# An adaLN mixer and mixture of experts on one core: z projection as split products, and every engine's step of the mixer in a new order

## The chip, the cores and the metric

The kernel runs on one core of a Trainium2 chip. A core has TensorE (matmuls into PSUM), VectorE, ScalarE and GpSimd, which run programs of their own and wait for each other by semaphores, and SyncE, which issues most DMA transfers. The metric is the device time of one execution in microseconds. Before the change the median of three runs was 5845.8 us (5838.91 to 5846.02).

## The reference, cut to what matters

Four sequences of 2048 tokens, width 512. Each token passes a state space mixer with a gate and then a mixture of 64 experts, eight per token, with one shared expert.

```python
h = _layernorm(x) * (1 + ca) + sa
xn = h * rsqrt(mean(h * h) + EPS) * norm_w
zxbcdt = xn @ in_proj_w.T             # z: 1024, xBC: 1024 + 2 * 128, dt: 16
conv = sum(pad[:, k:k + l, :] * conv_w[:, k] for k in range(4)) + conv_b
xBC = conv * sigmoid(conv)            # -> xs, B, C
dt = softplus(dt + dt_bias)
y = ssd(xs * dt, dt * A, B, C) + D * xs    # chunks of 128 tokens, a state carried from chunk to chunk
y = y * (z * sigmoid(z))
x = x + ga * (rmsnorm(y) * gnorm_w) @ out_proj_w.T
h2 = _layernorm(x) * (1 + cb) + sb
scores = sigmoid(h2 @ w_router)       # best 4 of 8 groups, best 8 experts
x = x + gb * (experts(h2) + shared(h2))
```

All arithmetic is fp32 in effect. Where the kernel wants fp32 quality at less TensorE work it splits both operands into a high and a low part of type fp32r and sums three products (high by high, high by low, low by high); the expert blocks did so before already, by the helper `split_products` (L1240).

## The kernel before, in words

The program has three parts. The function `mixer` walks over 64 chunks of 128 tokens and writes, per chunk, the residual `x1`, the normalised rows `h2` with their routing weights, and the lists of tokens per expert. In its spare moments it also splits one expert's weights per chunk into high and low parts. A short part builds tables from the lists. Then the expert blocks and a closing pass run.

In `mixer` each engine has a written-out `step`, called once per pass by `steps` (L493). One pass works on several chunks at once: `e` is the chunk two ahead (layer norm, `h`), `f` one ahead (the projections, the convolution, softplus of dt), `c` the current one (decay matrix `lm`, the products of the chunk, the state, the output product), `t` the last (`h2`, routing), `q` the one before (its list written). The order of the lines in `step` is the order of the engine's queue, so what waits at one line holds back all lines behind it on that engine; there is no scheduler.

A step of TensorE (L759 to L888) is: small products of `c` (L766), transposes of `xr` of `f` (L775), row sums of the decay matrix (L788), the xBC projection in four groups with dt (L811, L815), with the transposes of `h2` of `t` (L795) in between, the router (L825), the product inside the chunk `ydiag` (L832, 16 small matmuls), the product with the state `yoff` (L844), the new states (L853), the z projection (L860, eight fp32 matmuls of 512 columns), the transposes of `y` (L867), the two matmuls that rank the picked experts (L874), the transposes of xBC (L881) and the output product (L888).

VectorE multiplies `lm` by the masked B-C product (L956; the mask stands in PSUM, `half(4)`), applies three of four taps of the convolution (L982; ScalarE does the first), computes softplus as a series, and routes (L998 to L1037): a sigmoid's rest, best groups, best experts, up to `picked` (L1033), on which the rank matmuls wait. The series of softplus is laid between routing's operations. Then follow the sum of `y`, the gate, the state (L1043 to L1059), dt, the gate of z (L1086), the rank's keys, the split of weights (L518) and `x1` (L1109) with the statistics of its layer norm.

GpSimd (L580 to L654) forms `xg` (the gated `h` plus x), the reciprocal roots of both layer norms (`rs`, by a power) with the shifts `nm`, `xt` by the skip weights, `h2` and `h` (two operations each), the scaled rows `x2s`, the decayed state `tmp_s`, the scale `rr`, eight indirect DMAs that write the token list, and `r2`. SyncE's queue loads x and weights and stores x1, h2 and the split weights.

## Time and profile before

| what | value |
|---|---|
| median of three runs | 5845.8 us |
| profiled execution, its own time | 5848.36 us |
| its span from first to last instruction | 5846.6 us |
| mixer, 70 to 2640 us: TensorE busy | 2482.57 of 2570 us |
| VectorE, ScalarE, GpSimd busy in it | 2267.28, 1471.72, 1759.42 us |
| granted TensorE clock in it | 1.00 |
| expert blocks, 2700 to 5800 us: TensorE busy | 3031.78 of 3100 us |

"Busy" is the time in which an engine has at least one instruction in work; matmuls overlap, so that their starts tell more of their pace than their durations.
### The profile page before, as it was taken

How to read it: one execution, taken by the hardware profiler on the slowest of the kernel's cores; microseconds unless marked ns; L12 is line 12 of the kernel's file. 1: busy time of each engine (PE TensorE's matmuls, PEld its weight loads, DVE VectorE, ACT ScalarE, POOL GpSimd, SP SyncE). 2: the span in 40 equal slices, each digit the busy share in tenths (PEclk: the TensorE clock that was granted, in tenths of full speed). 3: DMA queues.
4: the chain of work that ended last, by engine and by line, in shares of the span. 5: the costliest groups of instructions: out<-in, count | busy, mean ns of one | idle time of the engine just before them, and what ended most of it. 6: DMA issues, size and time to landing. Idle time of an engine off the chain costs nothing.

```text
span 5846.6 us, 109797 instructions
## 1 busy us (share of the span) xinstructions
PE 5613.9 (96%) x28797; PEld 4286.0 (73%) x28798; DVE 3597.2 (62%) x10033; ACT 2627.2 (45%) x5588; POOL 3535.2 (60%) x2980
## 2 busy tenths in 40 slices
PE   5999999999999999994999999999999999999999
PEld 3666666666666666663888888887888888888887
DVE  4889888888898898883444444443444444444454
ACT  3555555555555555551333333333333333333322
POOL 2667667667676676673555555554555555555587
PEclk8999999999999999996999999999999999999999
DMA  5443444444444444343688788778678778878687
GB/s 203 163 149 144 162 155 152 154 143 163 158 145 165 147 146 160 145 151 133 138 225 222 183 202 224 164 177 238 138 182 203 160 161 218 208 199 201 132 277 248
DMA packets 340193, 1028.38 MB, mean 176 GB/s; under 512 B 57109, under 2 KB 61461, under 8 KB 339173
## 3 DMA queue, kind: packets, MB, share of 16 engines
q1 hardware_dynamic: 194232, 703.53, 32.9%
q0 software_dynamic: 145568, 321.56, 28.1%
q8 instruction: 118, 1.93, 0.1%
q14 instruction: 131, 1.07, 0.1%
q10 hardware_dynamic: 144, 0.29, 0.0%
HBM read 580.45 MB, written 444.74 MB: 175 GB/s over the span
## 4 chain that ended last, share of the span: by engine, by line
PE 52%; DMA 1%; POOL 0%; issue 0%; DVE 0%; SPq 0%; ACT 0%; POOLq 0%; ACTq 0%
PE bank L1244 45%; PE bank L1379 4%; PE bank L1386 2%; PE bank L1573 0%; PE bank L1582 0%; DMA w_lo<-lo_dram 0%; POOL acc_c L1555 0%; DMA h_c<-h_dram 0%; DMA lst_i<-list_dram,row 0%; DMA xg_e<-h_dram,ids 0%; POOL o_c L1559 0%; POOL acc_c L1546 0%; DMA acc_dram<-y_e,ids 0%; POOL lst_i L1172 0%; SPq L1531 0%
## 5 line engine op out<-in xcount | busy, mean ns | idle before, releaser
L1360 POOL DMA_INDIRECT acc_dram<-y_e,ids x576 | 910.4, 1580 | 1113.1 <-ACT y_e L1432 789.1
L1244 PE MATMUL bank<-w_hi,x_hi 128*128 (+1 forms) x2560 | 1056.1, 413 | 1.7 <-DVE x_lo L1647 1.2
L1244 PE MATMUL bank<-w_hi,x_lo 128*128 (+1 forms) x2560 | 1000.8, 391 | 0.0
L1244 PE MATMUL bank<-w_lo,x_hi 128*128 (+1 forms) x2560 | 1000.7, 391 | 0.0
L1450 DVE TENSOR_TENSOR h_lo<-bank,h_hi 128x256 fp32r<-128x256 f32 x576 | 243.8, 423 | 763.9 <-ACT h_hi L1421 763.7
L1432 ACT ACTIVATE y_e<-bank,xg_e 128x512 f32<-128x512 f32 x576 | 396.4, 688 | 698.4 <-PE bank L1244 698.4
L645 POOL DMA_INDIRECT list_dram<-tok_id,pos x512 | 594.9, 1162 | 156.0 <-issue 154.8
L1352 POOL DMA_INDIRECT xg_e<-h_dram,ids x576 | 571.0, 991 | 193.9 <-issue 174.9
L1426 ACT ACTIVATE th_f<-bank 128x256 f32<-128x256 f32 x576 | 221.3, 384 | 1011.2 <-PE bank L1244 1011.2
L811 PEld LDWEIGHTS bank<-xn_t,w_in 128*128 128x128 f32 x5120 | 587.8, 190 | 67.0 <-ACT btok L687 65.4
L811 PE MATMUL bank<-xn_t,w_in 128*128 128x131 f32 x5120 | 605.4, 276 | 14.8 <-ACT btok L687 14.1
L1459 DVE SCALAR_TENSOR_TENSOR hs_f<-th_f,bank 128x256 f32<-128x256 f32 x576 | 242.7, 421 | 600.1 <-ACT th_f L1426 599.8
L1244 PEld LDWEIGHTS bank<-w_hi,x_lo 128*128 128x128 f32 x2560 | 481.3, 188 | 103.5
L1244 PEld LDWEIGHTS bank<-w_hi,x_hi 128*128 128x128 f32 x2560 | 482.8, 189 | 83.4 <-DVE x_lo L1647 1.4
L1244 PEld LDWEIGHTS bank<-w_lo,x_hi 128*128 128x128 f32 x2560 | 484.1, 189 | 79.1
L982 DVE SCALAR_TENSOR_TENSOR acc<-bank,conv_w,acc 128x128 f32<-128x128 f32 x1920 | 505.7, 341 | 8.5 <-ACT acc L701 8.4
L1244 PE MATMUL bank<-w_hi,h_hi 128*128 (+1 forms) x1280 | 499.5, 390 | 2.2 <-DVE h_lo L1450 1.3
L1244 PE MATMUL bank<-w_hi,h_lo 128*128 (+1 forms) x1280 | 500.0, 391 | 0.0
L1244 PE MATMUL bank<-w_lo,h_hi 128*128 (+1 forms) x1280 | 498.1, 389 | 0.0
L888 PE MATMUL bank<-w_out,y_t 128*128 128x512 f32 x1024 | 452.4, 595 | 1.2 <-ACT y_t L751 1.2
L860 PE MATMUL bank<-w_in,xn_t 128*128 128x512 f32 x1024 | 450.0, 592 | 0.9 <-DVE acc L982 0.9
L1455 DVE TENSOR_TENSOR x_lo<-bank,x_hi 128x512 fp32r<-128x512 f32 x576 | 392.1, 681 | 8.7 <-ACT x_hi L1416 8.7
(247 smaller groups left out, 10448.6 us busy)
## 6 DMA issues: line engine op xcount, KB each, us to landing
hi_dram<-w_hi_m SPq DMA_DIRECT2D x130, 768.0 KB, 3.3
lo_dram<-w_raw SPq DMA_DIRECT2D x130, 768.0 KB, 4.8
w_hi<-hi_dram SPq DMA_DIRECT2D x130, 768.0 KB, 7.4
w_lo<-lo_dram SPq DMA_DIRECT2D x130, 768.0 KB, 10.2
w_raw<-in_w_experts_dram SPq DMA_DIRECT2D x128, 768.0 KB, 5.0
acc_dram<-zeros SPq DMA_DIRECT2D x130, 256.0 KB, 2.8
acc_c<-acc_dram SPq DMA_DIRECT2D x128, 256.0 KB, 3.5
h_dram<-h SPq DMA_DIRECT2D x64, 288.0 KB, 4.1
```

What stands on the lines that cost most here:

```text
L645: pool.indirect_dma_start(list_dram, bass.IndirectOffsetOnAxis(ap=pos[:, p, k:k + 1], axis=0), tok_id[:, p:p + 1], None).then_inc(list_st[ ...
L811: last = nc.tensor.matmul(raw_of(i), w_in[:, k, m:m + P], xn_t[:, k, :], start=(k == 0), stop=(k == KD - 1))
L860: last = nc.tensor.matmul(half(j), xn_t[:, k, OLD:], w_in[:, k, j * 512:(j + 1) * 512], start=(k == 0), stop=(k == KD - 1))
L888: last = nc.tensor.matmul(half(7), y_t[:, i, :], w_out[:, i, :], start=(i == 0), stop=(i == KI - 1))
L982: last = stt(out=acc[:, i, :], in0=raw_of(i)[:, k:k + P], scalar=conv_w[:, i, k:k + 1], in1=acc[:, i, :], op0=ALU.mult, op1=ALU.add)
L1244: last = nc.tensor.matmul(acc, a, b, start=(i == 0), stop=(i == len(terms) - 1))
L1352: pool.indirect_dma_start(xg[:, r, :], None, h2_dram, bass.IndirectOffsetOnAxis(ap=ids[:, r:r + 1], axis=0)).then_inc(g_in[r], 16)
L1360: pool.indirect_dma_start(acc_dram[r % NACC], bass.IndirectOffsetOnAxis(ap=ids[:, r:r + 1], axis=0), y[:, r % YSLOTS, :], None, compute_op ...
L1432: nc.scalar.activation(y[:, r % YSLOTS, :], half(6 + r % 2), ACT.Copy, scale=xg_flat[:, bass.ds(e + (r * ROW + DM), 1)]).then_inc(S["y_sb" ...
L1450: nc.vector.tensor_tensor(h_lo[:, r, :], half(4 + r)[:, 0:KF * P], h_hi[:, r, :].bitcast(FP32), ALU.subtract).then_inc(S["hT_lo"], 1)
L1455: nc.vector.tensor_tensor(x_lo[:, r, :], half(r), x_hi[:, r, :].bitcast(FP32), ALU.subtract).then_inc(S["xT_lo"], 1)
L1459: nc.vector.scalar_tensor_tensor(out=hs[:, r, :], in0=th[:, r, :], scalar=1.0, in1=half(2 + r)[:, 0:FF], op0=ALU.add, op1=ALU.mult).then_i ...
```

## The change

The z projection leaves the fp32 matmuls. At set-up `wz_hi` and `wz_lo` are made from the z columns of the weights; per chunk ScalarE copies `xn_t` to `xn_hi`, VectorE subtracts to get `xn_lo`, and TensorE runs 24 matmuls of 512 columns in two halves of 12 (L1324 in the changed kernel). The product of the mask goes from PSUM to a tile in SBUF, `cbm`. A pass now spans one chunk more: the first half of the xBC projection of `e` is done at the end of a pass and the second half at the start of the next; `x1` is finished, for `t`, at the head of the pass after its output product; the list's positions are for `q`. On every engine and in SyncE's queue the lines of `step` stand in a new order. `mod` is cut into three tiles with loads of their own. All taps but the first stay on VectorE (`K1 = 1`).

TensorE, from the product inside the chunk on. Before (`state` marks yoff, `x2s` the new states, `w_in,xn_t` z):

```order
L832 MATMUL bank<-x1s,lm 128x64 x16
L844 MATMUL bank<-state,xbc 128x512 x2
L853 MATMUL bank<-x2s,btok 128x512 x2
L860 MATMUL bank<-w_in,xn_t 128x512 x8
L867 MATMUL bank<-ident,y 128x128 x8
L874 MATMUL bank<-picked,tri_bf 128x64
L875 MATMUL bank<-picked,ones_bf 128x64
L881 MATMUL bank<-ident,xbc 128x128 x8
L888 MATMUL bank<-w_out,y_t 128x512 x8
```

Now (the rows ahead of these are z's second half, `wz` and `xn`):

```order
L1324 MATMUL bank<-wz_hi,xn_lo 128x512
L872 MATMUL bank<-x1s,lm 128x64 x16
L879 MATMUL bank<-picked,tri_bf 128x64
L880 MATMUL bank<-picked,ones_bf 128x64
L885 MATMUL bank<-ident,xr 128x128 x4
L893 MATMUL bank<-x2s,btok 128x512 x2
L902 MATMUL bank<-xn_t,w_in 128x131 x12
L908 MATMUL bank<-ident,y 128x128 x8
L914 MATMUL bank<-xn_t,w_in 128x131 x12
L919 MATMUL bank<-dta,tri 128x16
```

The rank matmuls (`picked`) moved from behind z and the transposes of `y` to right behind `ydiag`, and z stands ahead of `ydiag`.

VectorE at the start of routing. Before (`sc` is routing's first operation, `sp_a` the last before it):

```order
L991 TENSOR_TENSOR sp_x<-bank,dt_bias 128x16
L993 SCALAR_TENSOR_TENSOR sp_a<-sp_x 128x16
L998 TENSOR_SCALAR sc<-trt 128x64
L1000 TENSOR_TENSOR swb<-sc,b_router 128x64
L911 TENSOR_SCALAR sp_r<-sp_u 128x16
L1004 MAX g<-swb 128x8 x8
```

Now (`xn_t` is the carry of the taps):

```order
L1066 SCALAR_TENSOR_TENSOR sp_a<-sp_x 128x16
L1069 TENSOR_SCALAR tok_id<-tok_id 128x1
L1071 TENSOR_TENSOR key<-key,picked 128x64
L1073 MAX kmax<-key 128x8
L1076 TENSOR_SCALAR pos<-kmax 128x8
L1080 TENSOR_TENSOR lm<-lm,cbm 128x1024
L1086 TENSOR_TENSOR y<-bank,eacs 128x1024
L1089 TENSOR_SCALAR etk<-eacs,ends 128x16
L1092 SCALAR_TENSOR_TENSOR gz<-gz,bank 128x512
L1097 TENSOR_SCALAR xn_t<-xn_t,starts 128x4x3
L1101 TENSOR_SCALAR sc<-trt 128x64
L1103 TENSOR_TENSOR swb<-sc,b_router 128x64
```

Between softplus and routing there now stand the list's positions, one `lm` product, `y`, half a gate and the carry.

GpSimd, a step from the shifts on. Before (`rs`, `nm` twice: for `h2` and for `h`):

```order
L601 TENSOR_TENSOR xt<-xt,d_skip 128x1024
L607 TENSOR_TENSOR h<-hn,mod 128x512
L609 TENSOR_TENSOR h<-h,mod 128x512
L613 TENSOR_TENSOR rs<-ve,minus_half 128x1
L615 TENSOR_SCALAR nm<-mv,rs 128x1
L619 TENSOR_TENSOR h<-hn,mod 128x512
L621 TENSOR_TENSOR h<-h,mod 128x512
L627 TENSOR_TENSOR x2s<-x1s,eacs 128x1024
L633 TENSOR_TENSOR tmp_s<-state,etk 128x1024
L638 TENSOR_SCALAR rre<-ssq 128x1
L640 TENSOR_TENSOR rr<-rre,minus_half 128x1
```

Now:

```order
L637 TENSOR_TENSOR rs<-ve,minus_half 128x1
L639 TENSOR_SCALAR nm<-mv,rs 128x1
L646 TENSOR_TENSOR h<-hn,mod_b 128x512
L648 TENSOR_TENSOR h<-h,mod_b 128x512
L655 TENSOR_TENSOR h<-hn,mod_a 128x512
L657 TENSOR_TENSOR h<-h,mod_a 128x512
L660 TENSOR_TENSOR xt<-xt,d_skip 128x1024
L664 TENSOR_SCALAR rre<-ssq 128x1
L666 TENSOR_TENSOR rr<-rre,minus_half 128x1
L671 TENSOR_TENSOR x2s<-x1s,eacs 128x1024
L674 TENSOR_TENSOR tmp_s<-state,etk 128x1024
```

`xt` moved behind both `h`, the second shift ahead of `h2`, and `x2s` and `tmp_s` behind the scale `rr`, which now is directly ahead of them; the eight list DMAs come next.

```diff
+        w_in = sb("w_in", [P, KD, XBC + NH])
+        wz_hi = sb("wz_hi", [P, KD, DI], FP32R)
+        wz_lo = sb("wz_lo", [P, KD, DI], FP32R)
...
+        cbm = sb("cbm", [P, P])
...
+                    sp.dma_start(mod_a[:].rearrange("p m d -> p (m d)"),
+                                 mod_dram[0:1, 0:2 * DM].broadcast_to([P, 2 * DM])).then_inc(s_bcast, 16)
+                    sp.dma_start(mod_b[:].rearrange("p m d -> p (m d)"),
+                                 mod_dram[0:1, 3 * DM:5 * DM].broadcast_to([P, 2 * DM])).then_inc(s_bcast, 16)
                     for b in range(2):
-                        sp.dma_start(mod[:, b, :, :].rearrange("p m d -> p (m d)"),
...
-                        nc.scalar.activation(w_in[:, k, 0:DIN // 2], w_in[:, k, 0:DIN // 2], ACT.Copy,
+                        nc.scalar.activation(wz_hi[:, k, :], wz_raw[:, k, :], ACT.Copy,
...
+                    for k in range(KD):
+                        dve.wait_ge(s_act_set, 5 + k)
+                        nc.vector.scalar_tensor_tensor(out=wz_lo[:, k, :], in0=wz_raw[:, k, :], scalar=norm_w[:, k:k + 1],
+                                                       in1=wz_hi[:, k, :].bitcast(FP32), op0=ALU.mult, op1=ALU.subtract)
...
                         for dram in acc_dram:
                             sp.dma_start(rows_of(dram, ws), zeros[:, 0:DM]).then_inc(s_zero, 16)
+                    if t is not None:
+                        sp.wait_ge(S["x1_done"], t + 1)
+                        sp.dma_start(rows_of(x1_dram, t), x1[:, 1 - p, :]).then_inc(x1_st[1 - p], 16)
+                    if ws is not None:
                         split_load(sp, ws, 1)
+                    if ws is not None:
                         split_store(sp, ws, 0)
...
+                    if ws is not None:
+                        split_store(sp, ws, 1)
...
+                    if ws is not None and ws < NSET - 1:
+                        split_load(sp, ws + 1, 0)
...
-                    if c is not None:
-
-                        pool.wait_ge(S["x1s_done"], c + 1)
-                        nc.gpsimd.tensor_tensor(heads(xt[:]), heads(xt[:]), per_head(d_skip[:]),
-                                                ALU.mult).then_inc(S["xd_done"], 1)
...
+                    if t is not None:
+                        pool.wait_ge(S["hn2_done"], t + 1)
+                        at_least(pool, h2_st[1 - p], 16 * (t // 2))
+                        at_least(pool, S["h2T_ps"], t - 1)
...
+                        nc.gpsimd.tensor_tensor(h2[:, 1 - p, 0:DM], hn2[:], mod_b[:, 1, :], ALU.mult).then_inc(S["h2_half"], 1)
+                        pool.wait_ge(S["h2_half"], t + 1)
+                        nc.gpsimd.tensor_tensor(h2[:, 1 - p, 0:DM], h2[:, 1 - p, 0:DM], mod_b[:, 0, :], ALU.add).then_inc(S["h2_done"], 1)
...
                     if c is not None:
-
+                        pool.wait_ge(S["x1s_done"], c + 1)
+                        nc.gpsimd.tensor_tensor(heads(xt[:]), heads(xt[:]), per_head(d_skip[:]), ALU.mult).then_inc(S["xd_done"], 1)
+                    if e is not None:
+                        wait_apart(pool, S["ssq_done"], e + 1, passed)
+                        at_least(pool, S["xr_done"], e)
+                        nc.gpsimd.tensor_scalar(rre[:], ssq[:], DM * LN_EPS, None, ALU.add).then_inc(S["rr_var"], 1)
+                        pool.wait_ge(S["rr_var"], e + 1)
+                        nc.gpsimd.tensor_tensor(rr[:], rre[:], minus_half[:], ALU.pow).then_inc(S["rr_done"], 1)
+                    if c is not None:
                         pool.wait_ge(S["x1s_done"], c + 1)
                         pool.wait_ge(S["exps"], c + 1)
...
+                    if f is not None:
+                        act.wait_ge(S["xnT_sb"], f + 1)
+                        at_least(act, S["z_ps"], 2 * f)
+                        nc.scalar.copy(xn_hi[:], xn_t[:, :, OLD:]).then_inc(S["xn_hi"], 1)
...
+                    if f is not None:
+                        pe.wait_ge(S["taps"], XGROUPS * f + 2)
+                        pe.wait_ge(S["xn_lo"], f + 1)
+                        split_products(nc, half(0), [lambda k, t=t: t[:, k, :] for t in (xn_hi, xn_lo)],
+                                       [lambda k, t=t: t[:, k, 0:512] for t in (wz_hi, wz_lo)], KD).then_inc(S["z_ps"], 1)
...
+                    if f is not None:
+                        pe.wait_ge(S["taps"], XGROUPS * f + 1)
+                        pe.wait_ge(S["xn_lo"], f + 1)
+                        split_products(nc, half(1), [lambda k, t=t: t[:, k, :] for t in (xn_hi, xn_lo)],
+                                       [lambda k, t=t: t[:, k, 512:1024] for t in (wz_hi, wz_lo)], KD).then_inc(S["z_ps"], 1)
...
+                    if t is not None:
+                        pe.wait_ge(S["picked_done"], t + 1)
+                        if t + 1 < NCH:
+                            pe.wait_ge(S["yoff_sb"], t + 2)
+                        nc.tensor.matmul(half(6)[:, 0:EXPERTS], tri_bf[:], picked[:], start=True, stop=True)
+                        nc.tensor.matmul(half(6)[:, EXPERTS:2 * EXPERTS], ones_bf[:], picked[:], start=True, stop=True).then_inc(S["rank_ps"], 1)
...
                             for k in range(KD):
-                                last = nc.tensor.matmul(half(j), xn_t[:, k, OLD:], w_in[:, k, j * 512:(j + 1) * 512],
-                                                        start=(k == 0), stop=(k == KD - 1))
-                            last.then_inc(S["z_ps"], 1)
...
-
-                        at_least(dve, S["z_ps"], 2 * f)
-                        ts(xn_t[:, :, 0:OLD], xn_t[:, :, P:P + OLD], col(starts, f), None, ALU.mult).then_inc(S["carry"], 1)
...
+                    if f is not None:
+                        dve.wait_ge(S["xn_hi"], f + 1)
+                        at_least(dve, S["z_ps"], 2 * f)
+                        tt(xn_lo[:], xn_t[:, :, OLD:], xn_hi[:].bitcast(FP32), ALU.subtract).then_inc(S["xn_lo"], 1)
...
-                    if c is not None:
-                        for j in (1, 0):
-                            dve.wait_ge(S["l_exp"], 2 * c + 2 - j)
-                            tt(heads(lm[:, j * DI:(j + 1) * DI], 8, P), heads(lm[:, j * DI:(j + 1) * DI], 8, P),
-                               half(4)[:, 0:P].unsqueeze(1).to_broadcast([P, 8, P]), ALU.mult).then_inc(S["m_done"], 1)
+                        dve.wait_ge(S["l_exp"], 2 * c + 1)
+                        dve.wait_ge(S["cb_done"], c + 1)
+                        tt(heads(lm[:, 0:DI], 8, P), heads(lm[:, 0:DI], 8, P),
+                           cbm[:].unsqueeze(1).to_broadcast([P, 8, P]), ALU.mult).then_inc(S["m_done"], 1)
...
+                    if f is not None:
+                        dve.wait_ge(S["z_th"], 2 * f + 1)
+                        stt(out=gz[:, 1 - p, 0:512], in0=gz[:, 1 - p, 0:512], scalar=1.0,
+                            in1=half(0), op0=ALU.add, op1=ALU.mult).then_inc(S["gz_done"], 1)
+                    if e is not None:
+                        at_least(dve, S["z_ps"], 2 * e)
+                        at_least(dve, S["xn_hi"], e)
+                        ts(xn_t[:, :, 0:OLD], xn_t[:, :, P:P + OLD], col(starts, e), None, ALU.mult).then_inc(S["carry"], 1)
...
+                        at_least(dve, S["m_done"], 2 * f)
+                        tt(cbm[:], half(4)[:, 0:P], tri[:], ALU.mult).then_inc(S["cb_done"], 1)
```

## Rows read from the trace of the kernel before

**Rows 1.** TensorE in order of time: start us, us, line, operation, records, idle before.
```profile
1347.53 1.09 PE L867 MATMUL bank<-ident,y 128*128 128x128 f32 x8 [0.62 <-DVE y L1056]
...
1348.94 1.09 PE L881 MATMUL bank<-ident,xbc 128*128 128x128 f32 x8 [0.25 <-DVE xbc L1059]
1349.87 7.03 PE L888 MATMUL bank<-w_out,y_t 128*128 128x512 f32 x16
...
1357.90 3.60 PE L788 MATMUL bank<-lm,above 128*128 128x512 f32 x8
1361.72 8.37 PE L811 MATMUL bank<-xn_t,w_in 128*128 128x131 f32 x72 [0.22 <-ACT btok L687]
...
1370.36 1.07 PE L811 MATMUL bank<-xn_t,w_in 128*128 128x131 f32 x8
...
1372.07 1.08 PE L825 MATMUL bank<-w_router,h_t 128*128 128x64 f32 x8
1372.99 3.74 PE L832 MATMUL bank<-x1s,lm 128*128 128x64 f32 x32
...
1380.05 7.03 PE L860 MATMUL bank<-w_in,xn_t 128*128 128x512 f32 x16
1387.71 1.09 PE L867 MATMUL bank<-ident,y 128*128 128x128 f32 x8 [0.62 <-DVE y L1056]
```

**Rows 2.** TensorE in order of time in an expert block: first and tenth split matmul.
```profile
3603.11 0.39 PE L1244 MATMUL bank<-w_lo,x_hi 128*128 x1
...
3605.17 0.39 PE L1244 MATMUL bank<-w_lo,x_hi 128*128 x1
```

**Rows 3.** GpSimd in order of time in the same step.
```profile
1358.49 1.27 POOL L587 TENSOR_TENSOR xg<-h,mod 128x512 f32<-128x512 f32 x1 [6.55 <-DVE x L1111]
...
1361.06 1.61 POOL L594 TENSOR_TENSOR rs<-ve,minus_half 128x1 f32<-128x1 f32 x1
...
1366.33 2.67 POOL L609 TENSOR_TENSOR h<-h,mod 128x512 f32<-128x512 f32 x1
1368.95 0.54 POOL L613 TENSOR_TENSOR rs<-ve,minus_half 128x1 f32<-128x1 f32 x1
1369.70 0.27 POOL L615 TENSOR_SCALAR nm<-mv,rs 128x1 f32<-128x1 f32 x1 [0.21 <-POOL rs L613]
...
1375.34 1.90 POOL L633 TENSOR_TENSOR tmp_s<-state,etk 128x1024 f32<-128x1024 f32 x1
```

**Rows 4.** VectorE in order of time in the same step.
```profile
1361.06 1.21 DVE L949 TENSOR_TENSOR x1s<-xt,dt 128x1024 f32<-128x1024 f32 x1
...
1362.61 2.35 DVE L956 TENSOR_TENSOR lm<-lm,bank 128x1024 f32<-128x1024 f32 x2 [0.20 <-ACT lm L691]
...
1375.80 1.47 DVE L993 SCALAR_TENSOR_TENSOR sp_a<-sp_x 128x16 f32<-128x16 f32 x1
1377.19 0.18 DVE L998 TENSOR_SCALAR sc<-trt 128x64 f32<-128x64 f32 x1
...
1381.08 0.19 DVE L1033 TENSOR_SCALAR picked<-msr 128x64 bf16<-128x64 f32 x1
...
1382.90 1.22 DVE L1047 TENSOR_TENSOR y<-y,bank 128x1024 f32<-128x1024 f32 x1
```

**Rows 5.** One line over all chunks: ns min/median/max, first and last start.
```profile
L993 DVE SCALAR_TENSOR_TENSOR sp_a<-sp_x x64: 174/1474/1578, 95.4 to 2622.8; 128x16 f32<-128x16 f32 x64
```

**Rows 6.** A stretch: length, busy TensorE, weight load, VectorE, ScalarE, GpSimd; clock, DMA.
```profile
2673.00:2677.00 4.00, 2.15 (x11) 1.93 (x12) 2.35 (x11) 1.36 (x2) 0.00 (x0) 0.64 0.19 74
```

**Rows 7.** TensorE in order of time in the last chunk's step.
```profile
2673.85 1.75 PE L867 MATMUL bank<-ident,y 128*128 128x128 f32 x8 [4.46 <-DVE y L1056]
...
2676.71 9.23 PE L888 MATMUL bank<-w_out,y_t 128*128 128x512 f32 x16 [0.99 <-ACT y_t L751]
```

**Rows 8.** Start of the program: DMA issues of SyncE's queue.
```profile
56.53 0.81 SPq L248 DMA_DIRECT2D mod<-mod_dram  x2
66.46 0.81 SPq L537 DMA_DIRECT2D xin<-in_x_dram  x2
```

More of the change, by code:

```diff
@@ L369, in mixer @@
         RT = 3 * P
+        K1 = 1
         XGROUPS = 4
@@ L654, in step @@
                         nc.gpsimd.tensor_tensor(r2[:], r2e[:], minus_half[:], ALU.pow).then_inc(S["r2_done"], 1)
-                steps(pool, step)
+                steps(step)
                 for p in range(2):
@@ L818, in step @@
-                    if f is None and t is not None:
-                        transposes()
+                        if c + 1 < NCH:
+                            pe.wait_ge(S["taps"], XGROUPS * (c + 2))
+                            pe.wait_ge(S["dt_raw"], c + 2)
+                        else:
+                            pe.wait_ge(S["l_exp"], 2 * c + 1)
+                            at_least(pe, S["x1_done"], c)
+                        at_least(pe, S["state_done"], c)
+                        for j in range(2):
+                            last = nc.tensor.matmul(bank[3][:, j * 512:(j + 1) * 512], xbc[:, 9, :],
+                                                    state[:, j * 512:(j + 1) * 512], start=True, stop=True)
@@ new lines, in step @@
+                    if q is not None:
+                        at_least(dve, list_st[p], 16 * TOPK * (q // 2))
+                        ts(tok_id[:, p:p + 1], tok_id[:, p:p + 1], 2.0 * P, None, ALU.add)
+                        place.wait()
+                        place.mark(tt(key[:], key[:], picked[:], ALU.mult))
+                        place.wait_apart(passed)
+                        place.mark(nc.vector.max(out=kmax[:], in_=key[:]))
+                        place.wait()
+                        place.end()
+                        ts(pos[:, p, :], kmax[:], -1.0, float(KEY), ALU.mult, ALU.add).then_inc(S["pos_done"], 1)
@@ L1124, in tables @@
+                steps(step)
 def tables(nc, top, sem, tile, bank, half, env):
```

593 lines of the change are left out of this document (307 added, 286 removed).

## The prediction, made before the changed kernel was run

> **What bounds the kernel now.** I read the busy time by stretches first. It splits the run into the mixer, the tables and the expert blocks; the change touches the mixer alone, 64 chunks that follow each other in steps. Then I read one steady step engine by engine in order of time, and the waits with it. On TensorE [rows 1] the transposes of `y` begin at 1347.53 and again at 1387.71: the step is 40.18 us. In it TensorE waits three times, 0.62 us for the product `y`, 0.25 us for `xbc` and 0.22 us for `btok`, 1.09 us in all. The rest, 39.09 us, is matmuls end to end. So today a step is TensorE's own work plus a little; VectorE and GpSimd run beside it.
>
> What a reader should see next is how close those two sit, and that they stop each other. VectorE's `sp_a`, an operation of 128x16, takes 1.47 us and ends (1377.27) 0.03 us after GpSimd's `tmp_s` (1377.24) [rows 3, 4], and it does so at the median of all 64 chunks, against 0.17 us at the least [rows 5]. The other way round, GpSimd's 128x1 power at 1361.06 takes 1.61 us beside VectorE's `x1s` product, which starts in the same hundredth, where its twin takes 0.54, and one `h` operation 2.67 us, where the same shape takes 1.27 [rows 3, 4]. The VectorE operations in these pairs read two operands from SBUF. Those with one operand in PSUM, as the two `lm` products (2.35 us for both), run through GpSimd's work at full speed [rows 4]. Whichever starts first keeps the other out until it ends. All of my case hangs on this.
>
> **The change, part by part.**
>
> Work of TensorE. The z projection goes from 8 fp32 matmuls to 24 split ones. Before, they fill 1380.05 to 1387.09 (the next start less its wait), 7.04 us [rows 1]. The expert blocks run such split matmuls at (3605.17 - 3603.11) / 9 = 0.229 us each [rows 2], so 24 take 5.50 us. Everything else on TensorE stays in number and form. Its work per step becomes 39.09 - 7.04 + 5.50 = 37.55 us. If that were all, a step gained up to 2.6 us.
>
> Work beside it. ScalarE gains a copy of 128x512, VectorE a subtraction of 128x512 (about 0.7 us, as half a 128x1024 operation of 1.22 [rows 4]). Both stand at the start of a step, before matmuls that come later, and I cost them at nothing on the path: TensorE wants them for z, which comes 2.79 + 1.71 + 1.80 = 6.3 us into its step (the terms are under the first new wait). The order of the SP queue moves too: both stores of the split weights now stand ahead of the load of the next `x` rows and wait for VectorE's two split operations at the end of the step. What is queued behind them, the `x` rows of a chunk three steps on and a weight set of the next step, is wanted a quarter of a step later at the earliest; I cost it at nothing, and at one landing of a load if that cover went. GpSimd's eight list DMAs keep their place behind `tmp_s` and ahead of the scale `r2`, which the head of the next step wants. The causal mask now goes to a tile in SBUF, `cbm`; both `lm` products, 1.18 us each [rows 4], so read two SBUF operands and can hold GpSimd up or be held. The trace shows them only with PSUM. From below that costs nothing, from above 1.18 us each time; I take 1.18 for the first, since GpSimd starts `xg` just then, and let the second fall on work that does not decide. The Trainium skill, "SBUF — State Buffer", section "Who interferes with whom", states this as a rule: a VectorE instruction with two SBUF inputs contends with a GpSimd instruction that reads SBUF, one with fewer outside the fast modes does not. The trace agrees with it at both kinds of operand. By that rule the move of the mask is a cost, without it it is free.
>
> First new wait: transposes of `h2`. `x1` of a chunk now comes at the head of the next step, and TensorE wants `h2` after the output product, the `xbc` transposes (0.93 us), groups 2 and 3 with dt (12 of 36 in 8.37 us = 2.79; 1372.07 - 1370.36 = 1.71), two rows matmuls (half of 3.60) and z's first half (2.75): 9.98 us of cover [rows 1, 2]. Against it: from the output product's end at 1356.90 (1349.87 + 7.03) to GpSimd's start at 1358.49 1.59 us; from there to `h2` done at 1369.00 10.51 us today [rows 3]. In the new order the `xt` product leaves that chain (1.90, the size of `tmp_s`), so does the stall by the weight split (2.67 - 1.27 = 1.40); the other pair of small operations comes in (1368.95 to 1369.97, 1.02) and the stall by `lm` (1.18). That is 1.59 + 10.51 - 1.90 - 1.40 + 1.02 + 1.18 = 11.0 us. TensorE waits about 1.0 us, 0 to 1.5.
>
> Second new wait, the one that decides: the rank matmuls. Routing on VectorE now starts only after the whole z of the step has run, because the carry of the taps, which stands ahead of routing, waits for it. From z's end to routing's first operation I take 0.4 us (the semaphore and the carry), an estimate; from there to `picked`'s end it is 1381.08 + 0.19 - 1377.19 = 4.08 us [rows 4]. TensorE has only the 16 `ydiag` matmuls to cover that, about 3.6 us [rows 1], since the rank matmuls stand right behind them and the queue is in order: the transposes of `xr`, states, group 0, the transposes of `y`, group 1, the small ones and the output all stand behind. That is 0.9 us even with no stall. And GpSimd brings `x2s` and `tmp_s` there. Counted from `h2` done, GpSimd has two `h` operations (2.5), one stall by `lm` (1.2), `xt` (1.9) and a pair with a power (1.0), 6.6 us, before `x2s`; routing starts after the `h2` transposes (0.5, half of the eight of `xbc`), yoff (1.8, half of the rows matmuls), router (1372.99 - 1372.07 = 0.92), z (2.75) and 0.4, 6.4 us. They meet. Nearly every second operation of routing reads two SBUF operands. `x2s` and `tmp_s` are 1.90 us each, 3.8 together; VectorE advances in them by the operations with one operand, 1.3 us by my estimate (a third of routing's 4.08), so 2.5 us are lost. Bounds: 0, if they miss each other, to 3.8. I take 2.5. TensorE then waits 3.4 us for `picked`.
>
> Third: after `picked` VectorE still has 0.3 of routing, half a gate (0.6) and four operations of 1.2 us [rows 4], 5.7 us; TensorE has 5.2 (rank 0.2 by estimate, transposes 0.5, states 1.8, group 0 2.79). It waits 0.5 us at the transposes of `y`. The `dt` that the small matmuls want follows some 3 us later (`xbc`, at 1280 columns a quarter more than 1.22, and short ones), beside 0.93 + 2.79 us of TensorE's work: covered, by half a microsecond. The three waits of before (`y`, `xbc`, `btok`) are gone or counted here.
>
> Sum: 37.55 + 1.0 + 3.4 + 0.5 = 42.45 us a step, 2.27 more than before. With 61 steady steps (64 chunks without the first, in which nothing routes yet, and the last two) that is +138 us.
>
> Outside the steady steps. Of the ten rows that were broadcast before the first chunk six are left; the stretch from 56.53 to 66.46 [rows 8] shrinks by some 4 us. The two new setup loops on VectorE lie under the second load of `w_mod`. First and last chunks do the same operations one step apart from before; I leave them at what they took, with 10 us to either side.
>
> Against the profiled execution's own time: 5848.4 + 138 - 4 = 5982 us. That execution stood 2.6 us above the median of the runs, so I say 5980.
>
> **Rivals.**
>
> The clock. TensorE idles 0.62 us at most in a steady step today, and the granted clock is full. After 4.46 us of idling in the last steps it did fall: 0.64 over the next 4 us; the transposes of `y` took 1.75 us for 1.09, the output product 9.23 for 7.03 [rows 1, 6, 7], 2.9 us lost. A wait of 3.4 us in every step is nearer to that than to 0.62. If the clock (1.2 for 2.4 GHz) falls in most steps, each loses 2.9 less the 0.5 us wait that it swallows; in two of three steps that is 1.6 x 61 = +98, so 6080 us, in every step 2.4 x 61 = +146, 6128. The page "TensorE: Matmul & The Clock Gate" of the Trainium skill, section "HAM oscillation — how this bites in real kernels", warns of just such a loop: idle in each pass, half speed after. For it: the size of the wait. Against it: dense matmuls on either side.
>
> Faster. Two orders of things must hold at once: GpSimd stays clear of routing and of `lm`, so that the stalls vanish. Then the `h2` chain is 9.8 us and covered, the rank wait 0.9, the last 0.5: 38.95 us a step, -75 us, 5770. It turns at the point where the waits together are below 2.63 us (40.18 - 37.55). For it: TensorE's work does shrink by 1.5 us. Against it: `sp_a` [rows 5] shows that a tiny operation waits for the whole of `tmp_s`, and both `x2s` and routing hang on the same router matmul, so that they come together whatever else shifts.
>
> Nothing. Only the stall in routing is missing, the `h2` wait stays: 37.55 + 1.0 + 0.9 + 0.5 = 39.95, -14 us, 5830. It needs GpSimd late by two microseconds or more against the count above.
>
> That the split matmuls run no faster than fp32 in this stage I hold for excluded by [rows 2].
>
> **How the numbers follow.** Forecast 0.45, with its own range 5920 to 6060 (stall 1.5 to 3.8, a microsecond being 61 us of the run). Clock falls 0.22. Faster 0.15. Nothing, or near it, 0.18; of that a third inside a band of 0.2% to either side, about what a measurement of this kernel can tell from no change, and a third on each side of it. So faster 0.21, same 0.06, slower 0.73. The range 5800 to 6100 leaves out the faster case and the upper part of the clock's.
>
> **What would show it.** Right: the split matmuls near 0.23 us apart; the rank matmuls with 2 to 4 us idle before them, released by `picked`; `swb`, `gs` or `sp_s` on VectorE taking 1 to 2 us beside `x2s` and `tmp_s`; the `h2` transposes waiting for GpSimd; a step near 42.5 us. Wrong: routing's operations at their 0.15 to 0.25 us, `x2s` ending before routing starts, a step near 39 us with TensorE without gaps; or a granted clock well under 1 across the mixer, which is the first rival.

## The result, and the profile after

The changed kernel takes 6096.7 us, the median of four runs (6094.6 to 6101.3); the kernel before took 5843.8 us in the same session (5838.9 to 5846.0). The ratio is 1.0435, with a 95% interval of 1.0417 to 1.0453: 253 us slower. The forecast said slower, 5980 us, with 5920 to 6060 as its own range and 5800 to 6100 for all its cases: the time lies 37 us above the first range and inside the second by 3 us. The mixer's step is where it went: a step takes 44.35 us, from one start of VectorE's copy `acs` to the next, for 40.18 before, and 61 steps of 4.17 us more are 254 us.

```profile
1339.93 0.18 DVE L1195 COPY acs<-bank 128x32 f32<-128x32 f32 x1
...
1384.28 0.18 DVE L1195 COPY acs<-bank 128x32 f32<-128x32 f32 x1
```

First TensorE in order of time in one steady step (start us, us, line, operation, records, idle before), the answer to [rows 1]:

```profile
1355.17 0.40 PE L1324 MATMUL bank<-wz_lo,xn_hi 128*128 128x512 f32 x1
...
1357.50 0.40 PE L1324 MATMUL bank<-wz_hi,xn_lo 128*128 128x512 f32 x1
1358.09 0.66 PE L842 MATMUL bank<-ident,h 128*128 128x128 f32 x4 [0.20 <-POOL h L648]
...
1363.99 3.68 PE L872 MATMUL bank<-x1s,lm 128*128 128x64 f32 x32
1372.06 0.23 PE L879 MATMUL bank<-picked,tri_bf 128*128 128x64 bf16 x1 [4.39 <-DVE picked L1137]
...
1372.16 1.09 PE L885 MATMUL bank<-ident,xr 128*128 128x128 f32 x4
1373.05 3.62 PE L893 MATMUL bank<-x2s,btok 128*128 128x512 f32 x4
1376.46 2.97 PE L902 MATMUL bank<-xn_t,w_in 128*128 128x131 f32 x24
1379.27 1.04 PE L908 MATMUL bank<-ident,y 128*128 128x128 f32 x8
```

The split matmuls come 0.23 us apart, as [rows 2] said. One wait is left that counts: 4.39 us ahead of the rank matmuls, for `picked`. What follows it runs at about half speed: states take 3.62 us for the 1.88 of before, the transposes of `xr` 1.09 for 0.64. The same from 400 to 2600 us, in the mixer, waits first (us in total, times, longest), then a stretch with the granted clock in the third column from the right; before, that column was 1.00:

```profile
PE bank L879 <- DVE picked L1137: 215.7, 49, 4.5
PE bank L842 <- POOL h L648: 12.5, 49, 1.3
```

```profile
400.00:2600.00 2200.00, 1971.79 (x10781) 1458.39 (x10779) 2008.28 (x5305) 1179.97 (x2488) 1358.70 (x1237) 0.92 0.38 141
```

Now why `picked` is late: VectorE in the same step, the answer to [rows 4], and GpSimd beside it, the answer to [rows 3].

```profile
1348.05 0.75 DVE L1014 SCALAR_TENSOR_TENSOR x<-bank,r,mod_g 128x512 f32<-128x512 f32 x1 [2.11 <-PE bank L939]
...
1364.33 0.19 DVE L1101 TENSOR_SCALAR sc<-trt 128x64 f32<-128x64 f32 x1
1364.55 1.89 DVE L1103 TENSOR_TENSOR swb<-sc,b_router 128x64 f32<-128x64 f32 x1
1366.37 1.89 DVE L968 TENSOR_SCALAR sp_r<-sp_u 128x16 f32<-128x16 f32 x1
...
1371.60 0.40 DVE L1137 TENSOR_SCALAR picked<-msr 128x64 bf16<-128x64 f32 x1
```

```profile
1349.61 1.27 POOL L624 TENSOR_TENSOR xg<-h,mod_g 128x512 f32<-128x512 f32 x1 [13.59 <-DVE x L1016]
...
1353.06 0.54 POOL L631 TENSOR_TENSOR rs<-ve,minus_half 128x1 f32<-128x1 f32 x1
...
1360.57 2.96 POOL L660 TENSOR_TENSOR xt<-xt,d_skip 128x1024 f32<-128x1024 f32 x1
...
1364.46 1.90 POOL L671 TENSOR_TENSOR x2s<-x1s,eacs 128x1024 f32<-128x1024 f32 x1
1366.32 1.90 POOL L674 TENSOR_TENSOR tmp_s<-state,etk 128x1024 f32<-128x1024 f32 x1
```

`swb` and `sp_r` take 0.23 and 0.17 us in [rows 4]'s kernel and 1.89 each here; each ends with the GpSimd product beside it. Routing, from the start of `sc` to the end of `picked`, takes 7.67 us for 4.08.

The step can be added up as a loop: from `x` to GpSimd's start on `xg` 1.56 us; GpSimd's chain from there to the end of `tmp_s` 18.61 us; from there, through the rest of routing, to rank 3.84 us; and TensorE from rank to the next `x` 1348.05 + 44.35 - 1372.06 = 20.34 us. The sum is 44.35.

### The profile page after: what moved, and what is told of

It is laid out like the page before. It is cut to its first block, busy times and chain, and to the rows that moved or that the text cites. A ratio compares the mean times of both kernels' runs of the same rounds, so it can differ in the third digit from the quotient of the medians.

```text
span 6092.4 us, 111858 instructions
## 1 busy us (share of the span) xinstructions
PE 5647.6 (93%) x29309; PEld 4449.4 (73%) x29310; DVE 3899.0 (64%) x10101; ACT 2666.9 (44%) x5716; POOL 3498.8 (57%) x2980
## 4 chain that ended last, share of the span: by engine, by line
PE 49%; DMA 1%; POOL 0%; issue 0%; DVE 0%; SPq 0%; ACT 0%; POOLq 0%; ACTq 0%
PE bank L1324 43%; PE bank L1459 4%; PE bank L1466 2%; PE bank L1653 0%; DMA w_lo<-lo_dram 0%; PE bank L1662 0%; POOL acc_c L1635 0%; DMA lst_i<-list_dram,row 0%; DMA xg_e<-h_dram,ids 0%; DMA h_c<-h_dram 0%; POOL o_c L1639 0%; POOL acc_c L1626 0%; DMA acc_dram<-y_e,ids 0%; POOL lst_i L1252 0%; SPq L1406 0%
## 5 line engine op out<-in xcount | busy, mean ns | idle before, releaser
L1324 PE MATMUL bank<-w_hi,x_hi 128*128 (+1 forms) x2560 | 1055.4, 412 | 1.7 <-DVE x_lo L1727 1.2
L1324 PE MATMUL bank<-w_lo,x_hi 128*128 (+1 forms) x2560 | 1001.1, 391 | 0.0
L1324 PE MATMUL bank<-w_hi,x_lo 128*128 (+1 forms) x2560 | 1000.8, 391 | 0.0
L678 POOL DMA_INDIRECT list_dram<-tok_id,pos x512 | 519.4, 1014 | 147.8 <-issue 146.4
L624 POOL TENSOR_TENSOR xg<-h,mod_g 128x512 f32<-128x512 f32 x64 | 81.5, 1273 | 842.6 <-DVE x L1016 842.6
L1324 PEld LDWEIGHTS bank<-w_hi,x_lo 128*128 128x128 f32 x2560 | 481.3, 188 | 103.0
L1324 PEld LDWEIGHTS bank<-w_hi,x_hi 128*128 128x128 f32 x2560 | 482.9, 189 | 83.6 <-DVE x_lo L1727 1.4
L1324 PEld LDWEIGHTS bank<-w_lo,x_hi 128*128 128x128 f32 x2560 | 484.0, 189 | 79.1
L1324 PE MATMUL bank<-w_hi,h_hi 128*128 (+1 forms) x1280 | 499.1, 390 | 2.2 <-DVE h_lo L1530 1.3
L1324 PE MATMUL bank<-w_hi,h_lo 128*128 (+1 forms) x1280 | 499.9, 391 | 0.0
L1324 PE MATMUL bank<-w_lo,h_hi 128*128 (+1 forms) x1280 | 498.1, 389 | 0.0
L1459 PE MATMUL bank<-ident,xg_e 128*128 128x128 f32 x2304 | 346.3, 272 | 16.4 <-DMA xg_e<-h_dram,ids 8.0
L1496 ACT CAST x_hi<-bank 128x512 fp32r<-128x512 f32 x576 | 332.2, 577 | 65.7 <-PE bank L1459 65.6
L1459 PEld LDWEIGHTS bank<-ident,xg_e 128*128 128x128 f32 x2304 | 283.6, 140 | 96.3 <-issue 25.6
L1002 DVE SCALAR_TENSOR_TENSOR acc<-bank,conv_w,acc 128x128 f32<-128x128 f32 x1152 | 308.9, 343 | 15.8 <-ACT acc L713 10.2
```

The costliest lines, as they stand in the source:

```text
L678: pool.indirect_dma_start(list_dram, bass.IndirectOffsetOnAxis(ap=pos[:, p, k:k + 1], axis=0), tok_id[:, p:p + 1], None).then_inc(list_st[ ...
L1002: last = stt(out=acc[:, i, :], in0=raw_of(i)[:, k:k + P], scalar=conv_w[:, i, k:k + 1], in1=acc[:, i, :], op0=ALU.mult, op1=ALU.add)
L1324: last = nc.tensor.matmul(acc, a, b, start=(i == 0), stop=(i == len(terms) - 1))
L1459: last = nc.tensor.transpose(half(r % 2)[:, k * P:(k + 1) * P], xg[:, r, k * P:(k + 1) * P], ident[:])
L1496: nc.scalar.copy(x_hi[:, r, :], half(r)).then_inc(S["xT_hi"], 1)
```

## The experiments

Times are medians; differences are to the changed kernel's 6096.7 us, ratios to runs of the kernel before on the same chip.

**One of the two products away from routing.**

```
GpSimd, head of the step:  + tmp_s = state * etk        (was behind x2s)
VectorE, ahead of x1:      + etk = eacs * ends           (was ahead of the gate)
```

> The changed kernel, with one of the two GpSimd products that met routing (tmp_s) moved to the head of GpSimd's step, where GpSimd was idle for 13.6 us; the small product etk that it needs moves on VectorE to just before x1. Theory (VectorE stands still while GpSimd's x2s and tmp_s run, and TensorE's rank matmuls wait for that): one stall of 1.7 us of two goes (sp_r from 1.89 to about 0.2 us), routing takes about 6 us in place of 7.7, the rank wait falls from 4.4 to about 2.6, and the time is about 6097 - 61 x 1.8 = 5987; about 5870 if the shorter gap also keeps TensorE's clock up. Rival (TensorE waits because of where rank stands in its order, whatever GpSimd does): rank wait above 4 us, time 6080 to 6100. Second rival (the collision only changes its victim: tmp_s now stalls VectorE's taps): taps longer by 1.7 us, time 6080 to 6100.

Measured: 5982.3 us, ratio 1.0238 (1.0221 to 1.0255), 114 less. All engines in order of time:

```profile
1300.52 1.27 POOL L628 TENSOR_TENSOR xg<-h,mod_g 128x512 f32<-128x512 f32 x1 [1.55 <-DVE x L1021]
...
1315.38 1.90 POOL L675 TENSOR_TENSOR x2s<-x1s,eacs 128x1024 f32<-128x1024 f32 x1
1315.46 1.90 DVE L1105 TENSOR_TENSOR swb<-sc,b_router 128x64 f32<-128x64 f32 x1
...
1317.28 0.16 DVE L969 TENSOR_SCALAR sp_r<-sp_u 128x16 f32<-128x16 f32 x1
...
1321.14 0.20 PE L880 MATMUL bank<-picked,tri_bf 128*128 128x64 bf16 x1 [2.56 <-DVE picked L1139]
```

One stall is gone and the other is still there. The wait is 2.56 us, as the theory had it (2.6), and both rivals fall. GpSimd's chain from `xg` is 16.76 us for 18.61, and rank follows its end by 3.86 us, as in the changed kernel: 1.85 us a step, 113 us in 61 steps. The clock stays low (0.94 from 400 to 2600 us).

**Both away from routing.**

```
GpSimd:  h2 pair, x2s, xd, h pair, rr      (was: h2 pair, h pair, xd, rr, x2s, tmp_s; tmp_s as above)
```

> As the run with tmp_s early, and on GpSimd x2s and the product with D also go ahead of the pair that makes h, so that no large GpSimd product is left beside routing. Theory (the two GpSimd products are the whole stall): routing takes about 4.1 us, as in the kernel before, the rank wait is 0.8 to 0.9 us, TensorE's clock is full, and the time is about 6097 - 61 x (3.5 + 2.0) = 5760; 5880 if the clock stays low. Rival (h now comes 3.8 us later, so the rows xr for TensorE's transposes come late): the wait moves from rank to those transposes, 1 to 3 us, time 5900 to 6000. Rival (rank stands too early whatever GpSimd does): 6080 to 6100.

Measured: 5934.4 us, ratio 1.0155 (1.0138 to 1.0172), 162 less. Routing runs without a stall, 4.3 us, but the time is 54 us above the theory's more cautious number. VectorE in order of time, then GpSimd:

```profile
1371.76 1.92 DVE L1076 TENSOR_TENSOR key<-key,picked 128x64 f32<-128x64 f32 x1
1373.83 0.23 DVE L1078 MAX8 kmax<-key 128x8 f32<-128x64 f32 x1
1374.09 1.40 DVE L1081 TENSOR_SCALAR pos<-kmax 128x8 int32<-128x8 f32 x1
...
1378.27 0.89 DVE L1099 TENSOR_SCALAR xn_t<-xn_t,starts 128x12 f32<-128x12 f32 x1
```

```profile
1373.56 1.91 POOL L660 TENSOR_TENSOR xt<-xt,d_skip 128x1024 f32<-128x1024 f32 x1
```

The collision has moved ahead of routing: `key`, `pos` and `carry` take 1.92, 1.40 and 0.89 us, where the changed kernel has 1.28, 0.88 and 0.23. They stand on the same path, and the rank wait is still 2.03 us. `kmax`, a maximum, lies beside `xt` and is not held: 0.23 us, as without any GpSimd product beside it (placing early).

**Rank later on TensorE.**

```
TensorE:  ..., ydiag, xrT, states, group 0, yT, rank, group 1   (was: ydiag, rank, xrT, ...)
```

> The changed kernel with TensorE's two rank matmuls moved behind the transposes of y, nothing else. Theory (routing on VectorE is what is late, and y's three steps stand behind it there): no wait at rank, but y is done no earlier, so TensorE's transposes of y wait about 3 us in its place; the time is 6010 to 6090. Rival (only the place of rank in TensorE's order costs): the 4.4 us go, the clock comes back, and the time is 5750 to 5850.

Measured: 6031.5 us, ratio 1.0320 (1.0303 to 1.0337), 65 less: inside the theory's band, far from the rival's. TensorE's waits:

```profile
PE bank L896 <- DVE gz L1145: 163.4, 51, 3.5
PE bank L902 <- DVE state L1159: 27.5, 43, 1.8
```

The wait did not go. It went to group 0 of `xbc`, which needs the bank that the second gate frees, and VectorE comes to that gate behind routing (3.2 us a step), and to the transposes of `y` (0.5 us). I had the amount right and expected all of it at the transposes.

**The gap filled.**

```
TensorE, ahead of its wait for picked:  + 5 x matmul(half(6)[:, 128:512], tri, w_out[:, i, 128:512])
```

> The changed kernel with five matmuls of 384 fp32 columns, whose results nobody reads, on TensorE ahead of its wait for picked: the wait for routing stays, but TensorE works through some 3.3 us of it. Theory (a gap of 4.4 us costs a second time, because the clock is at its low level behind it: states 3.62 us in place of 1.88, the transposes of xr 1.09 in place of 0.64): states back at 1.9 us, the step shorter by about 2 us, time about 6097 - 61 x 2.0 = 5975. Rival (VectorE is the bound, and TensorE's slower matmuls are covered): the matmuls are fast again and the time stays at 6080 to 6100. Rival (the clock is not about the gap): states stays at 3.4 to 3.6 us and the time at 6100.

Measured: 6015.0 us, ratio 1.0293 (1.0276 to 1.0310), 82 less. Doing work that nobody needs makes the kernel faster. The same stretch as above:

```profile
400.00:2600.00 2200.00, 2098.18 (x11594) 1535.95 (x11594) 2061.95 (x5478) 1219.28 (x2572) 1390.45 (x1275) 1.00 0.39 144
```

The granted clock is 1.00, and states cost 0.593 us per matmul for 1.054. Of the 2 us a step that I gave the clock, 1.3 show in the time; 0.6 us turn into a wait for the state ahead of the transposes of `y`.

**z as before, new order.**

```
- split_products(half(h), xn_hi/xn_lo, wz_hi/wz_lo)    12 matmuls a half
+ 4 x matmul(half(h), xn_t, wz_hi as fp32)              4 fp32 matmuls a half
```

> The changed kernel in its new order, with z computed again by four plain fp32 products a half from the same places (the split of the input is still made, and its low part is not used). TensorE has 7.04 - 5.50 = 1.5 us more work a step. Theory (a step is a loop: VectorE from x1 to picked, 24.0 us, then TensorE from rank to the output projection, 20.2 us, and the z products lie outside of it, while VectorE works): the rank wait shrinks from 4.4 to about 2.9 us and the time stays at 6080 to 6110, or falls somewhat if the shorter gap keeps the clock up. Rival (TensorE's work sets the step): the time is 6097 + 61 x 1.5 = 6190.

Measured: 6100.5 us, ratio 1.0447 (1.0430 to 1.0465): 3.8 us more, not 94, and the interval overlaps that of the changed kernel. All engines in order of time:

```profile
1306.50 1.28 POOL L624 TENSOR_TENSOR xg<-h,mod_g 128x512 f32<-128x512 f32 x1 [13.58 <-DVE x L1018]
...
1321.95 1.30 DVE L1099 TENSOR_SCALAR xn_t<-xn_t,starts 128x12 f32<-128x12 f32 x1 [0.95 <-PE bank L868]
...
1323.17 1.93 POOL L674 TENSOR_TENSOR tmp_s<-state,etk 128x1024 f32<-128x1024 f32 x1
...
1325.11 0.16 DVE L970 TENSOR_SCALAR sp_r<-sp_u 128x16 f32<-128x16 f32 x1
...
1328.96 0.23 PE L881 MATMUL bank<-picked,tri_bf 128*128 128x64 bf16 x1 [3.54 <-DVE picked L1139]
```

The time is as expected, the way there only in part. z now ends later, so `carry` waits 0.95 us for it and routing starts later; but then `carry` and `swb` meet GpSimd in place of `swb` and `sp_r`, and VectorE is free at the same moment, the end of `tmp_s`. That is 18.60 us after `xg`, and rank comes 3.86 us behind it. In this order what ends routing is GpSimd's chain, not the end of z.

**The split products alone, old order.**

```
before.z:  fp32 products -> split products;  ScalarE + xn_hi (behind hn2);  VectorE + xn_lo (ahead of the taps)
```

> The kernel before, in its own order, with z as three split products (for want of SBUF the product of the high input part with the low weight part reads the high weights, so that this small term is left out); it adds one copy to xn_hi on ScalarE and one subtraction xn_lo of 0.68 us on VectorE just ahead of the taps. Theory of the loop (before, too, a step is VectorE from x1 to y, 1356.9 to 1387.7 = 30.7 us, then TensorE from the transposes of y to the output projection, 9.4 us; z lies beside it and xn_lo in it): TensorE's 1.5 us turn into a longer wait for y, and the time is 5846 + 61 x 0.7 = 5885. Rival (TensorE at 39.95 us of work in 40.18 is the bound): 5846 - 61 x 1.5 = 5755.

Measured: 5881.2 us, ratio 1.0070 (1.0053 to 1.0087): 40 us slower than before. TensorE's waits:

```profile
PE bank L877 <- DVE y L1070: 87.5, 54, 2.1
PE bank L855 <- DVE acc L996: 39.9, 54, 0.7
```

TensorE has 1.5 us less to do and waits 1.6 us for `y` (0.62 in [rows 1]) and 0.7 for the taps. The kernel before was not bound by TensorE's work either; its step is the loop of VectorE from `x1` to `y` and TensorE from there to the output.

**Placing early as well.**

```
VectorE, on top of both-away:  tok_id, key, kmax, pos  to just ahead of etk and x1   (was ahead of the second lm)
```

> As the run with all of GpSimd's large products ahead of routing, and VectorE's placing of the chunk before (tok_id, key, kmax, pos) is moved from just ahead of routing, where it took 3.7 us with its stalls, to the 1.9 us before x1 in which VectorE waits for the output projection. Theory (the loop from x1 to picked to the output projection sets the step): VectorE's part falls from 21.6 to some 18 us, picked is no longer waited for, TensorE becomes the bound with 37.6 us and small waits for xr and h2, a step takes 38 to 38.5 us, and the time is 5846 - 61 x 1.9 = 5730 (5700 to 5760). Rival (GpSimd's list transfers now start 11 us earlier and meet the next step's products, or xr becomes late by 1 to 2 us): 5800 to 5850.

Measured: 5929.6 us, ratio 1.0153 (1.0136 to 1.0169), 5 us less than without it. A miss: VectorE lost 3.7 us of work on that path and nothing came of it. VectorE in order of time:

```profile
1374.16 0.68 DVE L1094 SCALAR_TENSOR_TENSOR gz<-gz,bank 128x512 f32<-128x512 f32 x1
1376.71 1.25 DVE L1099 TENSOR_SCALAR xn_t<-xn_t,starts 128x12 f32<-128x12 f32 x1 [1.87 <-PE bank L1326]
1377.88 0.18 DVE L1103 TENSOR_SCALAR sc<-trt 128x64 f32<-128x64 f32 x1
```

Now VectorE arrives early and waits 1.87 us for the end of z, for `carry`, then is held for 1.0 us by the second `h` product. This is the tie that the forecast had named, routing behind `carry` behind z; the stalls had hidden most of it.

**Almost nothing of GpSimd beside routing, order untouched.**

```
- x2s, tmp_s: all 16 heads
+ x2s, tmp_s: head 0 only, the rest zeroed once
```

> The changed kernel in its own order; GpSimd computes x2s and tmp_s for one of the sixteen heads only (the other fifteen are left at zero), so that almost nothing of GpSimd meets routing. Theory (the stall of VectorE by these two products costs 3.6 us of VectorE's 24.0 us from x1 to picked, and the gap it makes costs the clock besides): routing takes about 4.1 us, the rank wait is about 0.8 us, states take 1.9 us again, a step takes 38.7 to 40.5 us, and the time is 5755 to 5860. Rival (the stall is beside the point, and TensorE waits for another thing by then): above 6000.

Measured: 5838.6 us, ratio 0.9996 (0.9986 to 1.0005), 258 less: the whole of the loss. In the changed order, with 3.2 us of GpSimd's work gone, the kernel stands where the kernel before did. All engines in order of time:

```profile
1333.49 0.28 DVE L1106 TENSOR_TENSOR swb<-sc,b_router 128x64 f32<-128x64 f32 x1
1333.64 0.29 POOL L674 TENSOR_TENSOR tmp_s<-state,etk 128x64 f32<-128x64 f32 x1
1333.69 0.28 DVE L971 TENSOR_SCALAR sp_r<-sp_u 128x16 f32<-128x16 f32 x1
...
1337.68 0.20 PE L882 MATMUL bank<-picked,tri_bf 128*128 128x64 bf16 x1 [1.08 <-DVE picked L1140]
```

Rank waits 1.08 us, the 0.9 of the forecast without a stall. The clock comes back only in part: 0.98 from 400 to 2600 us, states at 0.80 us per matmul.

**Routing untied from z.**

```
VectorE, on top of placing early:  carry  behind routing   (was ahead of it)
```

> As the run with placing early, and VectorE's small product that carries three columns of xn_t over (carry), which waits for the second half of z, goes behind routing; before that, routing stood behind it in VectorE's order and so could not begin until z was done (sc at 1377.9 us, with trt there from 1374.5 us). Theory (routing is tied to the end of z by carry alone): sc starts about 3 us earlier, but then runs beside GpSimd's two products for h, which were beside nothing, so routing takes 5 to 6.5 us; picked is late by 0 to 1.3 us in place of 2.0, and the time is 5800 to 5860. Rival (TensorE is the bound by now, or the wait only moves to the transposes of xr): 5900 to 5930.

Measured: 5839.1 us, ratio 0.9994 (0.9984 to 1.0004), 91 less than with `carry` ahead. Inside the theory's band, and the clock is 1.00 from 400 to 2600 us. TensorE's waits are now three small ones:

```profile
PE bank L843 <- POOL h L652: 53.1, 55, 1.6
PE bank L880 <- DVE picked L1135: 35.2, 55, 1.0
PE bank L903 <- ACT xn_t L795: 29.1, 55, 0.6
```

**xg early as well.**

```
xg: 2 buffers -> 3;  GpSimd: xg pair  to the head of the step, behind xn_lo;  wd in the tile of ms
```

> As the run with carry behind routing, and the two GpSimd products for xg, which had to wait for x1 because both use one of two buffers, get a third buffer and go to the head of GpSimd's step, beside VectorE's taps; to make room in SBUF, the routing weights wd share the tile of ms. All of GpSimd's other products then come some 3 us earlier. Theory (nothing of GpSimd is left beside routing, and routing is tied neither to z nor to x1): picked is there before TensorE wants it, TensorE's clock is full, its work of 37.6 us and small waits set the step, and the time is 5846 - 61 x 2.4 = 5700 (5680 to 5760). Rival (a new loop: with the products earlier, they meet VectorE's other steps ahead of routing, lm, x1s and key, and the loop from x1 to picked is as long as before): 5800 to 5860.

Measured: 5818.0 us, ratio 0.9961 (0.9947 to 0.9976): the best version, 0.4% faster than the kernel before, but 118 us behind the theory's 5700. VectorE in order of time:

```profile
1361.32 0.64 DVE L1100 TENSOR_SCALAR sc<-trt 128x64 f32<-128x64 f32 x1
1361.99 1.25 DVE L1102 TENSOR_TENSOR swb<-sc,b_router 128x64 f32<-128x64 f32 x1
```

Routing also starts earlier, so it meets `xd` and the first `h` product all the same: `sc` and `swb` 0.64 and 1.25 us. A step is 40.0 us (the taps start at 1340.71 and again at 1380.71), and in it VectorE stands idle in two places for more than 0.25 us, 0.32 and 1.30.

**The last collisions apart.**

```
VectorE: etk  into the first taps;   GpSimd: xd  behind picked
```

> As the run with xg early, with the last three collisions on VectorE's path taken apart: etk goes into the middle of VectorE's first taps, so that GpSimd's tmp_s lies beside taps and no more beside x1 (which took 1.43 in place of 0.69 us), and GpSimd's product with D (xd) goes behind picked, so that the products for h end 1.9 us earlier beside routing (sc, swb and gs took 2.35 in place of 0.6 us). Theory (a step is as long as VectorE's unbroken chain, 40.0 us, of which 2.5 us are stalls by GpSimd): 1.2 to 2 us of them go, a step takes 38 to 38.8 us, and the time is 5818 - 61 x 1.6 = 5720 (5700 to 5750). Rival (xd now comes late for y, and the list transfers behind it push r2 or xg): 5800 to 5850.

Measured: 5865.8 us, ratio 1.0042 (1.0028 to 1.0056): a miss, 48 us worse than without it; nearest to the rival, 16 us above its band. VectorE, then GpSimd:

```profile
1349.36 1.93 DVE L1145 SCALAR_TENSOR_TENSOR ms<-msr,sc 128x64 f32<-128x64 f32 x1 [0.19 <-issue]
```

```profile
1349.31 1.90 POOL L677 TENSOR_TENSOR xt<-xt,d_skip 128x1024 f32<-128x1024 f32 x1 [2.11 <-DVE picked L1144]
```

`xd`, released by `picked`, holds up the next operation of routing for its whole length, and the three steps of `y` stand behind that. TensorE then waits 1.8 us at the transposes of `y`. The run does not part its two moves: `etk`, now beside `xg`, takes 1.26 us for 0.23, more than the 0.74 us by which `x1` becomes shorter.

**The split products in that order.**

```
z: split products -> 4 fp32 matmuls a half, as above
```

> The kernel of the run before this one (tmp_s beside taps, xd behind picked), with z computed by four plain fp32 products a half again, 1.5 us more of TensorE a step: what the split products are worth once the order is mended. Theory (VectorE's chain from x1 to y is the step here too, and TensorE waits 2 us a step): the time is that of the run before this one within 25 us. Rival (TensorE's work now is the step): up to 61 x 1.5 = 94 us more.

Measured: 5863.6 us, ratio 1.0036 (1.0022 to 1.0049), 2 us from the run before it. The split products are worth nothing here either. With the best order, xg early, plain fp32 products were not run, so what the split is worth there stays open.

## Why the prediction was right in sign and short in size

**TensorE's work, 37.55 us a step.** Right. 44.35 - 4.39 - 0.20 leaves 39.76 us; less what ran at half speed (states 1.74, transposes of `xr` 0.45, group 0 0.10) it is 37.47.

**Transposes of `h2`, 1.0 us.** Measured 0.20: the count kept the 1.07 us by which `x1s` holds GpSimd's power up in [rows 3], and in the new order that power takes 0.54 us, without a stall. **Transposes of `y`, 0.5 us.** None: TensorE, slowed behind rank, came later than `y`. Together 1.3 us too much.

**Rank, 3.4 us.** Measured 4.39: the place, the releaser and the two products that cause it were right, and this is the term that was mis-sized. The step that failed is "VectorE advances in them by the operations with one operand, 1.3 us by my estimate". It does not advance. VectorE works in order, and the two operations at the head, `swb` and `sp_r`, were both held: `sp_r`, with one operand, waited 1.89 us for `tmp_s`, so that the loss is 1.66 + 1.72 = 3.4 us and not 2.5; without a stall it is the 0.9 of the forecast (1.08 in the run with one head). I had taken from the Trainium skill, "SBUF — State Buffer", section "Who interferes with whom", the sentence on two operands and left out its neighbour, that a `tensor_scalar` can also get into a mode that takes the shared port. The rows agree with that neighbour: 1.89 us for `sp_r`, 0.88 for `pos`, 0.89 for `carry` with all of GpSimd's products early; no row shows the mode itself.

**What the stall hangs on.** The forecast counted it from the end of z. The runs with one product moved and with fp32 z say otherwise: rank comes 3.84, 3.86 and 3.86 us behind GpSimd's last product, whether the chain is 18.6 or 16.8 us long and wherever z ends. GpSimd, busy for 57% of the span, was on the path. So the second stall by `lm`, which the forecast let fall on work that does not decide, lies on the path too: beside it `xt` takes 2.96 us for the 1.90 of before (what taking it away alone would give was not run). The tie to z's end is real but second; it was 0.69 us with one product moved and 1.87 us when the stall was gone (placing early).

**The clock.** This was a rival at 0.22, and it happened, in nearly every step (states take 1.054 us per matmul on average, 0.593 at full clock). By the rows it costs 2.3 us a step (forecast for it 2.4); filling the gap gave 82 us back, a third of the loss. I argued that dense matmuls on either side would hold the clock up; they did not. The section of the Trainium skill that the forecast named for this, "HAM oscillation — how this bites in real kernels" on the page "TensorE: Matmul & The Clock Gate", describes what came: a gap in each pass, half speed behind it (0.92 granted from 400 to 2600 us). A wait of 2.56 us already went with a clock of 0.94 (one product moved), so the forecast's own 3.4 us belonged with this rival: the two were one case. The rival's price for a fall in every step was 6128. Its 6080, for two steps in three, came nearer to 6096.7 by luck, because the `h2` and `y` terms were 1.3 us a step too high.

**Outside the steps, -4 us.** The stretch of [rows 8] lasts from 56.20 to 63.41 us now, 2.7 us less.

**The sum.** 42.45 - 0.8 - 0.5 + 1.0 + 2.3 = 44.45 against 44.35 measured.

**Reading before.** "Today a step is TensorE's own work plus a little" was the weakest sentence. TensorE was full and yet not what set the step: with 1.5 us less work a step became 0.7 us longer, by the subtraction of 0.68 us that came into VectorE's loop. The chance for faster rested on that saving, and in three pairs (old order, new order, the order of the last two runs) the split products bought nothing.

**Rivals.** Faster and Nothing needed GpSimd clear of routing. The run with one head made it so by leaving work out, and gave 5839, near the 5830 of Nothing but by another sum: its `h2` wait is 0.26 us and not 1.0, and the clock still falls in some steps.

## What to carry to other kernels

An engine that is nearly full need not be the bound: follow the loop of waits round once, add its pieces up to the step, and ask of each edit which piece it shortens. Before reordering, list every GpSimd product of two SBUF operands, and count its length as lost time for what VectorE does beside it with two SBUF operands, or as a `tensor_scalar` of eight or more columns. What read PSUM passed in these runs, and so did the maxima. Moving such a product pays where it comes to lie beside an idle VectorE or one that reads PSUM. A gap on TensorE that recurs in each step can cost twice, once as idle time and once at half clock behind it: here waits of 2 us and more did, waits of 0.6 us did not.
